# Attention over a fixed graph on one core: in each slot of TensorE's loop the scores of the row four ahead are issued before the present row's transposes and value product

## The reference, cut to what matters

```python
def reference(x, adj, Wq, bq, Wk, bk, Wv, bv, Wo, bo):      # x: 8 x 1024 x 256, adj: 1024 x 1024 of 0 and 1
    h = jnp.maximum(_layernorm(x, axis=-1), 0.0)
    q, k, v = (h @ Wq + bq), (h @ Wk + bk), (h @ Wv + bv)   # each split into 8 heads of 32
    scores = jnp.einsum('bqhd,bkhd->bhqk', q, k) / sqrt(32)
    scores = scores + (1.0 - adj)[None, None, :, :] * -1e9
    attn = jax.nn.softmax(scores, axis=-1)
    out = jnp.einsum('bhqk,bkhd->bqhd', attn, v).reshape(b, n, d)
    return x + (out @ Wo + bo)
```

## Time and profile before

| | before |
|---|---|
| device time, median of 3 runs (lowest to highest) | 1306.0 us (1303.83 to 1306.76) |
| span of the profiled execution | 1303.0 us |
| instructions | 30113 |
| PE, matmuls busy | 1240.9 us (95%) |
| PE, weight loads busy | 955.3 us (73%) |
| DVE busy | 994.4 us (76%) |
| ACT busy | 995.1 us (76%) |
| mean granted TensorE clock | 0.990 |
| DMA, 16 engines | mean 77 GB/s |

### The profile page before, as it was taken

One profiled execution on the slowest core, in us unless ns is written; L12 is line 12 of the kernel. 1 busy time (PEld: TensorE's weight loads), 2 busy tenths in 40 slices (PEclk: granted clock), 3 DMA queues, 4 the chain that ended last, 5 costly groups with the idle time before them and its releaser, 6 DMA issues.

```text
span 1303.0 us, 30113 instructions
## 1 busy us (share of the span) xinstructions
PE 1240.9 (95%) x10752; PEld 955.3 (73%) x10752; DVE 994.4 (76%) x1802; ACT 995.1 (76%) x1827; POOL 131.3 (10%) x234
## 2 busy tenths in 40 slices
PE   4799999999999999999999999999999999999998
PEld 4587776777777787777877777767877778778665
DVE  4697787877788777787878877887877878778775
ACT  2588876887877877777877878778777788778885
POOL 4002000020102101021010210002000020000001
PEclk9799999999999999999999999999999999999999
DMA  7442051512505133051421515124061320614001
GB/s 271 108 90 74 20 145 35 129 36 49 130 19 131 34 83 97 19 131 34 106 75 35 114 34 135 53 58 115 2 146 52 71 61 1 157 39 112 19 2 50
DMA packets 53470, 100.06 MB, mean 77 GB/s; under 512 B 10032, under 2 KB 35888, under 8 KB 53296
## 3 DMA queue, kind: packets, MB, share of 16 engines
q1 hardware_dynamic: 52720, 96.25, 29.4%
q0 software_dynamic: 576, 1.57, 0.5%
HBM read 22.28 MB, written 8.39 MB: 24 GB/s over the span
## 4 chain that ended last, share of the span: by engine, by line
PE 86%; ACT 7%; issue 3%; DVE 2%; SPq 1%; DMA 1%; POOL 0%; ACTq 0%; DVEq 0%; POOLq 0%
PE ps_turn L672 33%; PE ps_heads L727 18%; PE ps_scores L658 16%; PE ps_side L679 8%; PE ps_side L706 4%; PE ps_side L688 4%; ACT rows L411 4%; ACT turned_p L418 2%; SPq L241 1%; DVE turned_p L506 1%; PE ps_heads L714 1%; PE ps_turn L679 1%; ACT turned_p L424 1%; DVE q_lo L513 1%; ACT q_hi L429 0%
## 5 line engine op out<-in xcount | busy, mean ns | idle before, releaser
L495 DVE CUSTOM_DVE_ANT_0 rows<-ps_scores,mask 128x1024 f32<-128x1024 f32 x512 | 622.7, 1217 | 56.0 <-issue 31.7
L411 ACT ACTIVATE rows<-rows,row_min 128x1024 f32<-128x1024 f32 x512 | 590.6, 1154 | 29.9 <-DVE row_min L495 15.6
L672 PE MATMUL ps_turn<-ident,rows 128*128 128x128 f32 x4096 | 568.8, 277 | 28.4 <-issue 13.2
L672 PEld LDWEIGHTS ps_turn<-ident,rows 128*128 128x128 f32 x4096 | 458.6, 141 | 161.8 <-issue 82.9
L418 ACT ACTIVATE turned_p<-ps_turn 128x512 f32<-128x512 f32 x512 | 307.1, 600 | 227.9 <-PE ps_turn L672 226.5
L506 DVE COPY turned_p<-ps_turn 128x512 f32<-128x512 f32 x384 | 263.8, 687 | 199.3 <-PE ps_turn L672 197.7
L658 PE MATMUL ps_scores<-k_stack,q_stack 128*128 128x512 f32 x1024 | 365.8, 438 | 11.9 <-DMA k_stack<-k_lo 11.9
L727 PE MATMUL ps_heads<-turned_p,v 128*32 128x256 f32 x4096 | 248.7, 384 | 3.6 <-ACT turned_p L418 3.6
L727 PEld LDWEIGHTS ps_heads<-turned_p,v 128*32 128x32 f32 x4096 | 120.6, 110 | 105.4 <-ACT turned_p L418 24.6
L658 PEld LDWEIGHTS ps_scores<-k_stack,q_stack 128*128 128x128 f32 x1024 | 155.8, 193 | 14.2 <-issue 7.4
L388 POOL COPY inv_wide<-row_inv 128x256 f32<-128x256 f32 x64 | 25.5, 398 | 1092.0 <-DVE row_inv L542 989.6
(11 more groups left out here) (54 smaller groups left out, 474.8 us busy)
## 6 DMA issues: line engine op xcount, KB each, us to landing
k_stack<-k_hi SPq DMA_DIRECT2D x128, 128.0 KB, 2.4
k_stack<-k_lo SPq DMA_DIRECT2D x128, 128.0 KB, 2.4
q_stack<-q_lo SPq DMA_DIRECT2D x124, 128.0 KB, 2.4
q_stack<-q_hi SPq DMA_DIRECT2D x120, 128.0 KB, 2.4
res<-in_x SPq DMA_DIRECT2D x32, 256.0 KB, 2.8
out<-res SPq DMA_DIRECT2D x32, 256.0 KB, 2.2
xn<-in_x SPq DMA_DIRECT2D x7, 1024.0 KB, 5.8
mask<-in_adj SPq DMA_DIRECT2D x1, 3584.0 KB, 14.1
```

Source lines behind the costliest of these rows:

```text
L411: nc.scalar.activation(rows[:, m % RING, :], rows[:, m % RING, :], ACT.Exp, bias=row_min[:, m % RING:m % RING + 1], scale=-1.0, accum_out= ...
L495: nc.vector.tensor_tensor_reduce(out=rows[:, m % RING, :], in0=ps_scores[m % 2][:], in1=mask[:, qt, :], scale=1.0, scalar=START_MIN, op0=A ...
L672: tr = nc.tensor.transpose(bank[:, k, :], rows[:, i % RING, kt * P:(kt + 1) * P], ident[:])
```

## The change

Only PE's list changes. In each slot the block that issues `scores(n+4)`, with its wait for `masked`, moves from behind `turn(n)` to the front of the slot, ahead of `heads` and `turn(n)`. Nothing is added or removed, and the lists of DVE, ACT, POOL and SP are the same, instruction by instruction. With T for a row's transposes, S for the scores and X for side work, a slot was T(n) S(n+4) X(n) and is now S(n+4) T(n) X(n).

```diff
             def slot(b, g, i, first, last):
                 n, u = row(b, g, i), i // UNIT_ROWS
-                for half in range(2):
-                    if i % UNIT_ROWS == 0 and not (first and i == 0):
-                        heads(n, unit(b, g, u), g if u else 1 - g, half)
-                    turn(b, g, i, half)
                 m = ahead(g, i, SCORES_AHEAD)
                 if not (last and m >= BATCH_ROWS):
...
                     scores(m, row(b, 0, m), True, fills)
+                for half in range(2):
+                    if i % UNIT_ROWS == 0 and not (first and i == 0):
+                        heads(n, unit(b, g, u), g if u else 1 - g, half)
+                    turn(b, g, i, half)
                 if i % UNIT_ROWS == INV_ROW and not (first and i < HEAD):
                     turn_inv(unit(b, g, u))
```

## The result

The changed kernel takes **1330.2 us** (median of four runs, 1329.7 to 1331.5); the kernel before, on the same chip, 1306.3. The ratio is 1.019 (95% interval 1.018 to 1.021). The forecast was 1323.4, range 1305 to 1336.

What follows compares the result with a forecast made beforehand. PE was taken as the bound, with small holes in it. The terms 9.6 + 5.6 + 1.6 + 3.3 - 2.7 gave +17.4 us on the kernel before's 1306.0, so 1323.4 us, range 1305 to 1336.

Steps and rivals of the forecast that it cites:

- Price of a held slot: Any slot: loses 0.63 us less the slack, the time from the mask's end to the transposes' or value product's start.
- Part one: Slots 60 to 64, each batch's end: scores wait for masks, 8 x 1.2 = +9.6 us, bounds 5.0 and 12.
- Part two: Other slots with little slack: +5.6 us (21, 56 and similar) and +1.6 us (slot 26).
- Part three: Slot 3: scores no longer cover the projection's wait for `q_lo`, 7 x 0.47 = +3.3 us, bounds 0 and 3.3.
- the 0.7 that I had asked for: Slot 3: sign that PE's idle time at the wait becomes 0.7 us instead of 0.22.
- Part four: Side work's results come sooner, freeing T(42)'s half b behind slot 40: -2.7 us; sooner scores to DVE: 0.
- Part five: Jump back between slots 6 and 7: PE's idle hole changes nothing, 0 us, with +3.3 kept for the range.
- the sign that I had set on the hole: Jump back: the forecast is wrong if the hole changes by more than 0.5 us a round.
- for the same: Last batch's end, with no side work but the projection, was taken to lose 1.2 us like the other batches.
- absorbed: Rival: new holes fall into PE's existing waits at transposes; about +1 us, 1307; chance 0.12.
- faster: Rival: DVE, let go earlier, ends masks sooner and the shortage of slack vanishes; -5.7 us, 1300; chance 0.11.
- Worse: Rival: delays of transposes and masks feed each other in a loop of two rows; +29 us, 1335; chance 0.15.

Runs made afterwards that it cites:

- u_end_old: Changed kernel with the batch loop written out and the old order at slots 60 to 63 and 0: 1299.6 us, ratio 0.996.
- e_jump_old: Changed kernel with the old order in slots 7 and 8 only, the first behind the jump back: 1326.1 us, ratio 1.016.
- e_end_old: Changed kernel with the old order at slots 60 to 63 and slot 0 of the next batch: 1324.1 us, ratio 1.014.
- e_slack_old: Changed kernel with the old order in all 23 of 64 slots where a loss had been read: 1324.9 us, ratio 1.015.
- e_first_40_43: Kernel before with scores first in slots 40 to 43 only: 1304.6 us, ratio 0.999.

## Why the prediction was right, and where its sum was not

The direction, the case (the scores wait for the mask, at the end of each batch above all) and the range were right; the sum was 17.4 against 25.1 by the spans. Three things went wrong within it: the jump, which the sum had at 0, cost 5.5 us; a cover at slot 50 was missed; and the last batch loses in other places than was said. Errors the other way, 4 us in all, took back a part. Point by point:

**Price of a held slot: right.** Accumulator read to scores 0.06 (estimate 0.05), scores to T 0.57 (0.58). **Part one: right in cause and in the size of one end**, 1.05 us against 1.2 (1.12 given back in u_end_old), but seven ends pay it and not eight: 7.4 us against 9.6. Its steps: slot 60 costs nothing by itself, since in the old order DVE masked row 60 some 0.3 us late (0.65 us behind the start of slot 57, against 0.34) and in the new one it doesn't, so the mask that I took as fixed also moved. From slot 61 on the chain is as worked out, only 0.2 longer from T(62) to H(64): half of that is the copy, which starts 1.07 us behind T where 0.97 was taken (the rows before have 826.58 - 825.48 = 1.10), half the weight load of H.

**Part two: right in cause and about right in size**, 0.68 a batch at slots 11 to 22, 37 and 54 to 56 against 0.7, and 0.29 against 0.2 at slots 26 to 32. With the short mask these are all gone.

**Part three: right place, too large**, 0.32 against 0.47. The slot after the change, beside the earlier trace rows:

```profile
693.27 1.03 PE L672 MATMUL ps_turn<-ident,rows 128*128 128x128 f32 x8
693.33 0.68 ACT L429 ACTIVATE q_hi<-ps_side,bq_col 128x512 fp32r<-128x512 f32 x1
...
694.04 0.75 DVE L513 SCALAR_TENSOR_TENSOR q_lo<-ps_side,bq_col,q_hi 128x512 fp32r<-128x512 f32 x1
...
694.85 1.13 PE L706 MATMUL ps_side<-wo,heads_t 128*128 128x256 f32 x4 [0.55 <-DVE q_lo L513]
```

The projection starts 1.58 behind T(3); before it was 1.73. I had said that `q_lo` doesn't come sooner, since it hangs on the exponential ahead of `q_hi`. It comes 0.15 sooner relative to T(3). In the kernel before `q_hi` began 0.21 behind T(3), 0.03 behind the end of the q projection's last matmul; now the projection ends earlier and `q_hi` begins 0.06 behind T(3), right behind the exponential. These were the two rows:

```profile
680.98 0.69 ACT L429 ACTIVATE q_hi<-ps_side,bq_col 128x512 fp32r<-128x512 f32 x1
...
681.70 0.75 DVE L513 SCALAR_TENSOR_TENSOR q_lo<-ps_side,bq_col,q_hi 128x512 fp32r<-128x512 f32 x1 [0.22 <-ACT q_hi L429]
```

Then the scores' 0.47 come behind it: 0.47 - 0.15 = 0.32. PE's idle time, 0.55, is below the 0.7 that I had asked for.

**The same step missed elsewhere: slot 50.** A projection also follows T there, and `copy_v` clears its buffer:

```profile
813.06 0.69 DVE L520 TENSOR_TENSOR v<-ps_side,bv_row 128x512 f32<-128x512 f32 x1
...
813.80 0.73 PEld L706 LDWEIGHTS ps_side<-wo,heads_t 128*128 128x128 f32 x4 [0.31 <-DVE v L520]
```

The scores had covered this wait in full before, so no row of the waits showed it. The sum therefore lacks 0.35 x 7 = 2.4 us. I looked for lost cover only where a wait was already seen; a wait that is covered in full has no row, and must be found by asking for every side work what clears its buffer.

**Part four: right, a little small**, -0.48 a batch against -0.33. T(42)'s halves now stand together, eight in one piece and nothing idle ahead, beside the earlier trace rows:

```profile
790.58 0.69 ACT L429 ACTIVATE k_hi<-ps_side,bk_col 128x512 fp32r<-128x512 f32 x1 [2.46 <-PE ps_side L679]
...
792.40 1.03 PE L672 MATMUL ps_turn<-ident,rows 128*128 128x128 f32 x8
```

**Part five: wrong**, and the step that failed is "if the hole begins when PE's sequencer reaches the jump, nothing changes". There are six taken jumps, not seven rounds, and they cost 5.5 us; the bound of 3.3 was also too low. PE's hole itself hardly changed (2.06 to 2.40 us before, 2.11 to 2.59 after); what grew stands behind it, so the sign that I had set on the hole (0.5 us a round) was set on the wrong stretch. First the kernel before, then the changed one, same batch:

```profile
691.63 1.07 PE L672 MATMUL ps_turn<-ident,rows 128*128 128x128 f32 x8 [2.16 <-issue]
691.78 1.15 ACT L411 ACTIVATE rows<-rows,row_min 128x1024 f32<-128x1024 f32 x1 [2.58 <-issue]
...
692.54 1.22 DVE L495 CUSTOM_DVE_ANT_0 rows<-ps_scores,mask 128x1024 f32<-128x1024 f32 x1 [2.81 <-issue]
...
693.96 1.29 PE L727 MATMUL ps_heads<-turned_p,v 128*32 128x256 f32 x20
```

```profile
704.26 0.72 PE L658 MATMUL ps_scores<-k_stack,q_stack 128*128 128x512 f32 x2 [2.41 <-issue]
...
704.82 1.03 PE L672 MATMUL ps_turn<-ident,rows 128*128 128x128 f32 x8
...
705.92 1.22 DVE L495 CUSTOM_DVE_ANT_0 rows<-ps_scores,mask 128x1024 f32<-128x1024 f32 x1 [3.34 <-PE ps_turn L672]
...
707.07 0.08 DVE L495 DVE_READ_ACCUMULATOR2_ANT row_min<- 128x1 f32 x1
...
707.20 0.73 PE L658 MATMUL ps_scores<-k_stack,q_stack 128*128 128x512 f32 x2 [0.48 <-DVE row_min L495]
...
707.87 1.50 PE L727 MATMUL ps_heads<-turned_p,v 128*32 128x256 f32 x24
```

I had looked at PE's hole alone. DVE and ACT have their own at the same place, and DVE comes out of it with a mask still to do. Before, T(7) stood behind the jump and could go at once, H(8) 2.33 behind it. Now T(7) waits first for the 0.56 of scores, and the next scores, ahead of H(8), for the second mask: H(8) comes 3.05 behind T(7). This is the "held slot" of part one, at a place where the slack is small because DVE is late by its own jump. In every round of the changed kernel without a fall of the clock H(8) starts 1.95 us behind the start of DVE's first mask. (That mask, of row 10, does not wait for T(7), though the row names `ps_turn`: over the six rounds it begins 0.7 to 1.4 us behind T(7).) DVE's own hole is 3.1 to 3.5 us in the changed kernel and 2.6 to 3.3 in the kernel before; why it is longer is not shown. e_jump_old shows 4 us going away with these two slots, and in the pair without jumps the loss here is 0.

The clock can be set apart by rounds. From T(6) to slot 9 the rounds without a fall take 11.2 to 11.5 us in the kernel before (four rounds) and 12.2 to 12.4 in the changed one (three rounds), 0.95 more. Rounds with a fall take 12.8 and 12.9, and 13.1 to 13.4. So two falls of 1.5 us before stand against three of 1.0 after, and 6 x 0.95 = 5.7 is the order's own. In the table 2.1 is the round in which the clock fell in the changed kernel alone, and 0.3 and 0.4 are the rounds in which it fell in both.

**What "for the same" hid.** The last batch has no side work but the projection, and I took its end for the same. Its end is not: under `if not (last and m >= BATCH_ROWS)` its slots 60 to 63 issue no scores, so nothing is held there, and from slot 59 to the closing value product the changed kernel loses nothing (-0.1 us). But without side work the slack is small all along its second phase: slots 34, 42 and 50 cost 0.53 each, with the scores right behind the masks. It costs 3.9 in all, 1.7 more than the others, so the 1.2 us put at its end stand elsewhere, and that they are covered is luck.

**The sum again**, measured less forecast, in us: part one 7 x 1.05 - 9.6 = -2.2; part two 8 x (0.68 + 0.29) - 7.2 = +0.6; slot 3 7 x 0.32 - 3.3 = -1.1; part four -0.48 x 7 + 2.7 = -0.7; slot 50 +2.4; the jump +5.5; the rest of the last batch +2.6; the rest of batch 0 +0.6. Together +7.7, and 25.1 - 17.4 is 7.7.

Of the rivals, "absorbed" and "faster" fell with the first trace: the masks at 60 to 64 end where the slack said. "Worse" had the nearer time, 1335, but not the reason: the held slots did share their delay, and no loop of two rows formed; the excess came from slot 50, the jump and the last batch.

## What to carry to other kernels

Before moving a waiting instruction ahead in an in-order queue, read for each place how long before the queue's next work its producer had ended, and compare it with the length of the moved work; a place with less slack pays the difference, and here this gave 1.2 us for a measured 1.05 at each batch's end. Ask of each place whether the moved work is issued there at all: at the last batch's end it is not. Do the same for every wait that the moved work had covered, also those that no row shows since the cover was whole, and at a loop's jump for every engine that the moved work waits for, not for the bounding engine alone. With two buffers the distance has two sides here: scores first cost 1.9%, between the halves 1.3%, last 4.6%, and just behind the transposes, as before, was the best of the four.

## What the runs showed of the hardware

- **A taken jump is long on all three engines of the loop.** In the kernel before PE had idled 2.16 us ahead of its first transposes behind it, ACT 2.58 and DVE 2.81; PE's own record of the compare and branch is 3.4 to 3.9 us where it is taken, and 0.08 where it falls through at the last round. Writing the loop out gained 18 us of 1306, for six jumps 3 us each; by the traces 14.0 us stand at the jumps themselves and 3.2 at the two falls of the clock behind them, so it is not the instructions that the written-out kernel has fewer (27926 against 30113) that make the gain. Behind the start of each of the twelve taken branches in the two kernels' traces, 1.0 to 1.4 us later, a DMA queue of kind "instruction" moves 16 KB, landing by 2.6 us, and two more transfers of 8 KB follow; in the 4 us behind the branch that falls through there is none. The Trainium skill (Runtime: NRT & Kernel Launch, Instruction fetch mechanics) says that a taken branch to a page that isn't loaded makes the engine wait for it to be fetched; these runs agree: the taken jump alone is long, and instruction transfers stand in each of them. That the engines wait for these and nothing else is not shown.
- **The granted clock falls behind some of these holes.** Where PE had idled at the jump (2.29 us in the rows of e_end_old, then a stretch at 0.53), it fell in two rounds of six in the kernel before, three in the changed one and six in e_end_old; behind the hole of 2.41 us shown above for the changed kernel it did not. In the written-out kernels, which have no such hole, it was 0.993 to 0.995 over the execution, against 0.986 in e_end_old. The four runs of e_end_old have 0.985 to 0.989, those of the changed kernel 0.990 to 0.991, so its many falls are no chance of one execution. Why the old order at a batch's end goes with them stays open; I did not try to find out.
- **Edits of order in single slots don't add.** Each border between the two orders costs or gives about 0.46 us of scores, and gives it back only where PE isn't held (e_slack_old, e_first_40_43). An order should be judged over the whole round, from traces of that very order.
